# Three of eight key tiles of the full layers' value product as float32r pairs split on GpSimd, with feed normalisations and head splits on GpSimd too

## The chip, the cores and the metric

One Trainium2 chip, one core of it. The metric is the device time of one execution of the program in microseconds, lower is better. Every input is in float32 and the result is compared with a float32 reference.

## The reference

Four layers in a row work on `x` of 4 batches x 256 channels x 32 x 32 pixels, so 1024 tokens a batch.

```python
x = L0(x)   # gamma * attention(x) + x, q and k of 32 channels, v of 256
x = L1(x)   # x + wo(attention(group_norm(x))), q, k, v of 256 channels
x = L2(x)   # layer norm, causal attention with 8 heads of 32 and one shared k and v,
            # then layer norm, ff_w1, layer norm, gelu, ff_w2, residual
x = L3(x)   # as L1, with other weights
# attention of L0, L1 and L3 (the "full" layers), per batch:
scores = einsum('bci,bcj->bij', q, k) * scale      # 1024 x 1024
attn   = softmax(scores, axis=-1)
out    = einsum('bcj,bij->bci', v, attn)           # sum over 1024 keys j
```

## The kernel before, in words

Everything stays in SBUF. Three chains of work are woven together on every engine: the **full chain** (L0, L1 and L3 for four batches, 12 layers in all, in the order of the list `FULL`), the **causal chain** (the attention of L2 with its layer norm ahead) and the **feed chain** (L2's output product, norms and feed-forward part, in quarters of 256 tokens). A table of strings, `ORDER`, one per engine, says piece by piece which chain comes next: `F` or a digit is a piece of the full chain, `C` or a letter up to h of the causal one, `G` or a letter from i of the feed chain. On TensorE (the string `PE`) a digit or such a letter also names the PSUM bank of the eight in which the piece's result is put. A piece that opens a bank waits until the unit that held it has been read. The strings were put together ahead of time, nothing is decided at run time.

Most products are taken to float32 exactness by **pairs**: a float32 number is split into a float32r part (`hi`, rounded) and the rest (`lo`), and the product is three cheap float32r matmuls, hi x hi, hi x lo and lo x hi (`PASSES` and the helper `product`, line 758). ACT writes the hi part, DVE subtracts for the lo part. The attention's value product of a full layer is not done so, but as plain float32 matmuls, each of which the trace records as two instructions on TensorE (line 811, 768 in the program and 1536 in the trace).

A full layer goes, per query tile `ti` of 128 tokens: scores on TensorE (`full_scores`, two banks), row maximum on DVE (`row_max`, lines 1349 and 1352), exponential on ACT (`exponents`, line 1124), division on DVE (`invert`, line 1360), transposition on TensorE in two halves of four key tiles (`full_turn`, line 802, units t0 to t15), and copy of each half to `probsT` on ACT (`turned`, line 1132). After every second query tile comes a quarter of the values (`full_values`, units o0 to o3), which waits for the last of its four copies:

```python
for ct in range(CT):                      # 2 halves of the channels
    for j in range(NT):                   # 8 key tiles of 128
        last = mm(o[:, ct * QUARTER:(ct + 1) * QUARTER], vt[:, j, ct * P:(ct + 1) * P],
                  probsT[:, qi % (NQ - 1), j, :], start=j == 0, stop=j == NT - 1)
```

DVE then adds the quarter to the residual (`residual`, line 1370).

GpSimd (POOL) does 64 masks on the causal diagonal (`affine_select`, line 731) and 64 powers for the reciprocal roots of the norms (lines 710 and 720), nothing else of weight. DVE does the feed chain's normalisations (`norm_end` for the steps `f1b` and `f2b`, line 1557) and, as the third piece of `normalise`, divides a block of heads and splits it into a pair (lines 1672, 1675 and 1676).

Of the kernel before, what the change touches and what calls it, by code (L numbers as in the profile page):

```python
# [5 lines left out]
F32 = mybir.dt.float32  # L6
# [6 lines left out]
P = 128  # L13
# [28 lines left out]
        "0Fc4F60F2Fe50F72d5F401F756FFF3F750F26d7FFF0F2675d4FFF017FFF05F204F6F2046F012F405F710FFF2F456F012FFF3Ff70120F"  # L42
        "FF3F5F701F0FFF3fb3F53F705Fbh031F4h56FFF0F723fF6ah25dgFFaFbdfahce6F0123eegacd5gaFdFFbCaf71adeCgcbCe0jgdCfFFgF"
        "gdCjfpdbghCcjpeCc0ebCGceahce0cCdFC5kaC3f1F3fFfCakfaC5dakda5d5dfC1Fde76C3fCFb76nbC3Fgb5g1C2dfFdbFfdFfC2eFg04n"
        "gC6FcCGci4C50gCFcCFeCFgb2eCFg0C456pc0eFCcFCFhCC4CFcj6Fe03kj6Fa5GmFdFFgbh3if1F3ihf6F01kl4F2G6ad0F756FFcaehFca"
        "4F720Fd6e7caef7caFfFFdCca5F7301cfg3CaeFcnFCgFaf27Cd2FafpFaCFfalchfC6aeCa2F4o20Fe2gCFeo0ceGe2a5c0fCFgnC236fCF"
        "a520Flg52gClg3aFfpkCafFahGFfa2fFC0bfC14gCFca6C23eaFeCaFeageFaeC30ecFp5eCcC74cC2dCaC5FpFcCaepFcC0fCpkfF37fGC0"
        "fCFcC3CFCFfFmf2h22mF0pg246Fijcdf02dG6faFb034bF067FdbfaFdFb5F7adb03F56b7aFFdfFb2eF17gCe56c1FFhFc03eCg3FFcFbCe"
        "gaCdeoadCfahdcC4F0F64F0Fk64Fka67aC4F260F7e26ahCeFaeFhaFe0FcC62dCfC3F50jo2FFdFadCGac4F6aC23ae62FadeaFeCFga74C"
        "k0FbCFfFbCegibC6pe6F0ki64bGFg1aFe6beC16e1lgFdC764F3bC71oFoeC37e6CFpjcCFFGeC6bFa54bC6F5d12CFFF16dbCdFC512d4CC"  # L50
        "1FFFCg2Fie671dF0FpgFlF4dgamngd3G6adFb3505Fca74cfga2F4fgafhafa1f2FeCaf14af6cCFahFneCFca4cFC6a12eaFeC6i1ei6cbF"
        "feFCFcaC72aFgmib67C41Gc4gbFagFbFdC5bCFh4C3bm5F7bdCFbdFbCdFbdh13bd1fCF3afCaC15ibfC3bfFaCf2afa1fdfC1dfFp3eCfC7"
        "eCgCb4CopbCF36GibheCaCeCc0CgCFjCFoCF4Fop320F6Gm57FFF2F01m56p0FFjkF31G7FFF04F260F4F2604F326F014F326FFF0F724F3"
        "67FFF0F23456FFF707FFF"),
    "ACT": (
        "FFFFCFFFFFCCFFFCCFFFCCFFFFFFFFFCFFFFFCFFFFFFFFFFFFFFFFFFFFFFFFFFFCFFFFFFFFFFFFFCCFFFFFCCFFFFFFFFFFFFCCCCCCFC"
        "FFFFCCCCCFFCCCCCGCCCCGCGCCFFCCFFCFCFGCFFCFFCCCFFFCCFFFGCFFFCCCCFFFCGCFFFCCCCCCFFFFFFFCCCGCFCFCFGFFCGFGCFCFGF"
        "FFGFCCFFFFFCCCFFFCFFFCCCCCFFFFFCCCCFFCGCCCCFFFFGFCFFFCGFFCCCFFCFCFFGFFFFCGCGCCCFFFCCFFFCCCCCCCFFFFFFFCCGCCCC"
        "GCFFFCGCCCCFCFFGFFFFGFFFGCCCFFCFFFFCCCCCFFFFFFCCFFFFFCCFFCCCCCCCFFCFFFGFFFCFFFFFFFFFCCCCCCFFFGFFFCGCFFFFFCCC"
        "CFFCCCGFFFFGFCGFFFCFFCCFFFCGFFFCFFFCGCGCCFFFCCFFFCCCFFFFFFFCCFCFFCGFGCFGFCCCFFFFCFFCFCCCCFFFCCCFFFCCCCFFFCGF"  # L60
        "FFCCCCCGFFFFFFFGCCCCFFCFCCCFFFCCFCCFFFGCCCFFFCCCCFCCCFFGCGFCCCFCFCCGGFFFGFFFGFFFFFGFFGFFFFFFFFFFFFFFFFFFFFFF"
        "FFFFFFFFFF"),
    "DVE": (
        "CFFFFCFFFFFFCCFFCCFFCCCFFFFFFFCFFFFCFFFFFFFFFFFFFFFFFFFFFFFFFFFFFFCCFCFFFFFFFCCFFCCFFFFCCFCFFFFFCFFCCFCFFCCC"
        "CCFFCCCCCFFCCCCCCCCGGGCGGGCGCCGCCGGCCCGFFFCGCCFGCCFFCCFFFCCFGGGGGGFCGCCFFCGCFCFCCCGCCFGFGFCFFCGCFCCCCCFCCCFF"
        "FGGGGFGGGGCCCFFFFFCCGCFCCCFCGGFGCFGCGGGGCGGGCFGCCGCFGGFGFFGFFGFCCFCFCCCCCFFFFFFCCCCCFFFCFCCCCCCCGGGGGGFCGFCC"
        "CGCFCFFCFCCFFGFFFGCGFCGFCFFCCCFGFCCCFGGGFGGGFGFCGCFGGCGFCCGCCGFCCCFCFFCFFCCCCCCCFCFCCGGGFGGGFFGFFFFGCCCGGFGG"
        "CFCGCCCCCFGGGGGGFGCCGFFGGCFGFFCCGCCFGFCCFFCFCCCCFCFCFFCFCCFCFFCCCCCFCCCFCCCGCCCCCCFFGGGGFGFGFFGFFFGCFFGFFCGF"
        "CCCCCFCCFFFFGFFCCFCFCGFCCCCCCCFFGGGGGGGFCFFGFCFFGFFFGCGFCGFGCCFFCCFFCCCGGGFGGGFGFGFFGGFGGFCGCCFFFFFFFCCFFFFC"
        "FFFFCCCCFGGGCGGGCGCGGGFGCCCGCFGFFCCFCFFCCCCCFFCCCCFCFCCCCFCCCCGGGFGGGFGCCCFCFCGFCGGCCGCFFCFCFFFCGFCFFFCCGCCC"  # L70
        "FFGGGGGCCGCGCCFCCFCCCCFFFFCGCFCCCCCCFCCCFGGFGCCGCFGGGGFGGGGGGGCCGCFFGFFGGGGFGGGFGFGFGGGGFGFFFFFFFFFFFFFFFFFF"
        "FFFFFFFFFFFF"),
# [24 lines left out]
LN_SLOTS = 4  # L97

# [245 lines left out]
def build(nc, t):  # L344
# [38 lines left out]
    with ExitStack() as ctx:  # L383
# [36 lines left out]
        r_x, r_y, r_z, r_h, r_g, r_v, r_p, r_t = (region(k) for k in (8, 8, 8, 16, 16, 8, 8, 24))  # L420
# [124 lines left out]
        diag_masked = sem("diag_masked")  # L545
        full_step = sem("full_step")
# [151 lines left out]
        def _(pool):  # L698
# [3 lines left out]

            def full_chain():
                n = 0
                for l, b in FULL:
                    if l == "L0":
                        continue
                    n += 1
                    pool.wait_ge(gn_var_ready, n)
                    pool.tensor_tensor(gn_rstd[:, :], gn_var[:, :], half_neg[:, 0:CT], ALU.pow).then_inc(gn_rstd_ready, 1)  # L710
                    yield
# [32 lines left out]
        def _(pe):  # L744
# [61 lines left out]
            def full_values(l, b, qi):  # L806
                wait_read(pe, full_name(l, b, ("t", 4 * qi + 3)))
                o = open_unit(full_name(l, b, ("o", qi)))[:, 0, :]
                for ct in range(CT):
                    for j in range(NT):  # L810
                        last = mm(o[:, ct * QUARTER:(ct + 1) * QUARTER], vt[:, j, ct * P:(ct + 1) * P],  # L811
                                  probsT[:, qi % (NQ - 1), j, :], start=j == 0, stop=j == NT - 1)
                        if ct == CT - 1 and j == NT - 1:
                            last.then_inc(filled["f"], 1)
                        if j % TPH == TPH - 1:
                            yield
# [46 lines left out]
            def full_chain():  # L863
                for n, e in full_events():
# [25 lines left out]
                    else:  # L890
                        yield from full_values(l, b, e[1])
# [210 lines left out]
        def _(act):  # L1102
# [24 lines left out]
            def turned(l, b, ti):  # L1127
                for i in range(2 * ti, 2 * ti + 2):
# [3 lines left out]
                    nc.scalar.copy(probsT[:, ti // 2 % (NQ - 1), js, (ti % 2) * P:(ti % 2 + 1) * P],  # L1132
# [619 lines left out]
```

## Time and profile before

| | |
|---|---|
| time, median of 3 runs | 1383.28 us (1382.95 to 1383.52) |
| the profiled execution's own time | 1383.94 us |
| its span | 1382.2 us |
| TensorE's mean granted clock | 0.98 of 2.4 GHz |
| busy: PE, PEld, DVE, ACT, POOL | 1294.4, 1011.7, 846.2, 576.1, 92.2 us |
| idle time of PE | 1382.2 - 1294.4 = 87.8 us |

PE is TensorE's matmuls, PEld its weight loads (they overlap the matmuls). The duration of one matmul in the trace holds the way through the array, so that successive matmuls overlap: what one costs is the distance from its start to the next one's. The chain is the list of work, followed back from the last instruction, that set the end.

### The profile page before, as it was taken

To read this page: it belongs to the slowest core of one execution; us is meant where nothing else is said; L and a number is where in the kernel's file an instruction comes from. 1 tells how busy PE (TensorE), PEld (TensorE's weight loads), DVE (VectorE), ACT (ScalarE), POOL (GpSimd) and SP (SyncE) were. 2 spreads that over 40 slices of the span, in tenths; PEclk is the share of its full clock that TensorE was granted. 3 is DMA by queue.
4 is the path that set the end of the run, shared out by engine and by line. 5 is a ranking of instruction groups with operands and counts; after the bars stand their busy time and mean duration, and the time that the engine had idled before them with its cause. 6 is when DMAs were issued, how large, how long until landed. Compare 5 with 4: busy or idle time off the path is not lost.

```text
span 1382.2 us, 21753 instructions
## 1 busy us (share of the span) xinstructions
PE 1294.4 (94%) x8800; PEld 1011.7 (73%) x8800; DVE 846.2 (61%) x1886; ACT 576.1 (42%) x911; POOL 92.2 (7%) x134
## 2 busy tenths in 40 slices
PE   6979989899999898999999999999999999999898
PEld 5868777666768676776788767767787677668786
DVE  3634456787647757667477476676577676656451
ACT  3423343355343543544545245344435342453331
POOL 0000000110010001001100010001000000010000
PEclk9999999999999999999999999999999999999999
DMA  5000020110002000000020111000020101000000
GB/s 189 1 0 1 0 77 1 24 24 1 1 2 46 2 24 1 24 2 1 2 46 2 39 47 24 1 1 1 1 46 1 24 16 32 9 2 16 16 1 31
DMA packets 20610, 27.04 MB, mean 20 GB/s; under 512 B 3488, under 2 KB 14240, under 8 KB 20512
## 3 DMA queue, kind: packets, MB, share of 16 engines
q1 hardware_dynamic: 20512, 25.66, 6.6%
q8 instruction: 71, 1.16, 0.3%
q14 instruction: 27, 0.22, 0.1%
HBM read 8.61 MB, written 4.19 MB: 9 GB/s over the span
## 4 chain that ended last, share of the span: by engine, by line
PE 84%; DVE 8%; ACT 6%; issue 2%; DMA 1%; SPq 0%; ACTq 0%; DVEq 0%
PE ring L758 28%; PE ring L811 25%; PE ring L1062 10%; PE ring L1043 5%; PE ring L1026 4%; PE ring L802 4%; ACT probs L1124 1%; DVE part_max L1645 1%; PE ring L960 1%; PE ring L839 1%; PE ring L1030 1%; PE ring L995 1%; ACT probsT L1132 1%; DVE neg_max L1349 1%; DVE shift_max L1352 1%
## 5 line engine op out<-in xcount | busy, mean ns | idle before, releaser
L811 PE MATMUL ring<-probsT,vt 128*128 128x256 f32 x1536 | 359.7, 385 | 8.2 <-ACT probsT L1132 7.8
L811 PEld LDWEIGHTS ring<-probsT,vt 128*128 128x128 f32 x1536 | 287.5, 192 | 59.4 <-ACT probsT L1132 11.3
L1274 ACT ACTIVATE cprobs<-ring 128x1024 f32<-128x1024 f32 (+1 forms) x160 | 150.2, 941 | 252.5 <-PE ring L1043 251.5
L1124 ACT ACTIVATE probs<-ring,neg_max 128x1024 f32<-128x1024 f32 x96 | 107.0, 1115 | 148.0 <-DVE neg_max L1353 75.2
L1645 DVE TENSOR_REDUCE part_max<-ring 128x2 f32<-128x1024 f32 (+2 forms) x112 | 127.2, 1145 | 45.1 <-PE ring L1026 30.2
L1026 PE MATMUL ring<-ks,qs 96*128 96x512 f32 (+3 forms) x384 | 107.8, 379 | 11.1 <-DVE part_max L1645 4.1
L1043 PE MATMUL ring<-qs,ks 98*128 98x512 f32 x288 | 106.9, 443 | 9.8 <-ACT probs L1124 5.6
L1352 DVE TENSOR_REDUCE shift_max<-ring 128x1 f32<-128x1024 f32 x64 | 78.3, 1223 | 59.1 <-PE ring L758 57.0
L1132 ACT COPY probsT<-ring 128x512 f32<-128x512 f32 x192 | 101.9, 591 | 25.1 <-PE ring L802 25.1
L802 PE MATMUL ring<-consts,probs 128*128 128x128 f32 x768 | 107.6, 280 | 3.9 <-DVE probs L1360 1.5
L758 PE MATMUL ring<-h_hi,q_hi 128*128 128x512 f32 x256 | 107.4, 419 | 1.9 <-ACT vt L1146 0.7
L802 PEld LDWEIGHTS ring<-consts,probs 128*128 128x128 f32 x768 | 90.7, 144 | 23.6 <-issue 9.7
L758 PE MATMUL ring<-h_hi,q_lo 128*128 128x512 f32 x256 | 101.1, 395 | 0.0
L758 PE MATMUL ring<-h_lo,q_hi 128*128 128x512 f32 x256 | 100.6, 393 | 0.0
L1062 PE MATMUL ring<-cprobs,v 128*32 128x256 f32 (+1 forms) x1280 | 96.7, 374 | 0.1
L1062 PE MATMUL ring<-cprobs,ones 128*32 128x256 f32 (+1 forms) x1280 | 93.0, 362 | 0.0
L1026 PEld LDWEIGHTS ring<-ks,qs 96*128 96x128 f32 x384 | 61.6, 191 | 30.4 <-issue 7.4
L731 POOL TENSOR_SCALAR_AFFINE_SELECT cprobs<-cprobs 128x512 f32<-128x512 f32 x64 | 42.3, 662 | 558.5 <-ACT cprobs L1274 558.5
L1360 DVE TENSOR_SCALAR probs<-probs,row_inv 128x1024 f32<-128x1024 f32 x96 | 72.5, 756 | 3.4
L1043 PEld LDWEIGHTS ring<-qs,ks 98*128 98x128 f32 x288 | 49.2, 191 | 29.0 <-issue 15.3
L758 PEld LDWEIGHTS ring<-h_hi,q_hi 128*128 128x128 f32 x256 | 48.4, 189 | 19.5 <-issue 8.9
L1062 PEld LDWEIGHTS ring<-cprobs,v 128*32 128x32 f32 x1280 | 25.5, 108 | 45.9 <-issue 39.4
(226 smaller groups left out, 2110.1 us busy)
## 6 DMA issues: line engine op xcount, KB each, us to landing
qs<-q_hi SPq DMA_DIRECT2D x32, 128.0 KB, 2.3
qs<-q_hi SPq DMA_DIRECT2D x64, 64.0 KB, 2.0
x<-x_dram SPq DMA_DIRECT2D x3, 1024.0 KB, 6.1
qs<-q_lo SPq DMA_DIRECT2D x16, 128.0 KB, 2.3
qs<-max_rows SPq DMA_DIRECT2D x128, 2.0 KB
qs<-q_lo SPq DMA_DIRECT2D x32, 64.0 KB, 2.0
out_dram<-z SPq DMA_DIRECT2D x4, 512.0 KB, 2.8
out_dram<-x SPq DMA_DIRECT2D x4, 512.0 KB, 2.8
```

The source lines that it names most:

```text
L758: ins = mm(out, w, m, start=first and n == 0, stop=last and n == len(every) - 1)
L802: last = nc.tensor.transpose(o[:, j, :], probs[:, ti % 2, (TPH * hf + j) * P:(TPH * hf + j + 1) * P], ident)
L811: last = mm(o[:, ct * QUARTER:(ct + 1) * QUARTER], vt[:, j, ct * P:(ct + 1) * P], probsT[:, qi % (NQ - 1), j, :], start=j == 0, stop=j == ...
L1026: last = mm(o, stack(k, a, 3 * DH, at, at + P), ks[0:3 * DH, lo:hi], start=i % own == 0, stop=not diag and i % own == own - 1)
L1043: last = mm(heads(name)[:, a:a + own, 0:n], ks[0:3 * DH + 2, jt * P:(jt + 1) * P], stack(k, slice(a, a + own), 3 * DH + 2, QUARTER - n, QU ...
L1062: last = mm(acc[DH * a:DH * (a + 1), (half + 1) * QUARTER - n:(half + 1) * QUARTER], w, causal_probs(step, n)[:, a, :], start=jt == 0 and ...
L1124: A(probs[:, ti % 2, :], flat(full_name(l, b, ("s", ti))), ACT.Exp, bias=neg_max[:, ti:ti + 1], accum_out=row_sum[:, ti:ti + 1]).then_inc( ...
L1132: nc.scalar.copy(probsT[:, ti // 2 % (NQ - 1), js, (ti % 2) * P:(ti % 2 + 1) * P], slot(name)[:, 0, :].rearrange("p (s n) -> p s n", n=P)) ...
L1274: A(causal_probs(step, n), heads(name)[:, :, 0:n], ACT.Exp).then_inc(read_done[chain[name], "act"], 1)
L1352: full_then(v.tensor_reduce(shift_max[:, ti:ti + 1], flat(name), AX_X, ALU.max, negate=True))
L1360: v.tensor_scalar(probs[:, ti % 2, :], probs[:, ti % 2, :], row_inv[:, ti:ti + 1], None, ALU.mult).then_inc(probs_scaled, 1)
L1645: v.tensor_reduce(cols if ti < TPH else parts[:, ch, :], src[:, :, 0:n], AX_X, ALU.max, negate=True).then_inc(read_done["c", "dve"], 1)
```

## The change

1. In `full_values` the key tiles 3 to 7 stay plain float32 matmuls and come first; the key tiles 0 to 2 (`PAIRED = 3`) follow as pairs, three float32r matmuls each. Ahead of the first pair of a quarter TensorE waits for GpSimd's splits (`vt_split`, `probs_split`).
2. GpSimd makes these pairs: once a layer for `vt` (three key tiles, 768 numbers in a row of each partition), and once for each of the 8 query tiles for `probsT` (three key tiles, 384 numbers), always a copy that rounds to `hi`, a wait for it and a subtraction that writes `lo` over the source. It waits for ACT's copy of the first half of the query tile alone.
3. The normalisations `f1b` and `f2b` of the feed chain and the split of the divided heads go from DVE to GpSimd. (A function that would split the gelu there as well is defined and never called.)
4. The scratch tiles `turned_sums` and `den` are gone, both transpositions of `normalise` write to `nums`. `probsT` has two buffers in place of three.
5. The strings of `ORDER` are others, on all five engines.

```diff
 ORDER = {
     "PE": (
-        "0Fc4F60F2Fe50F72d5F401F756FFF3F750F26d7FFF0F2675d4FFF017FFF05F204F6F2046F012F405F710FFF2F456F012FFF3Ff70120F"
+        "0Fc4F60F2Fe50F72d5F401F760FFF3F516F021FFF3F0215ga1FFF027FFF03F513F5F0246F012F405F710FFF2F456F012FFF3fF70120F"
...
+PAIRED = 3
...
-        vt = shared("vt", [P, NT, C], r_v)
+        vt, vt_lo = (shared(n, [P, NT, C], r_v, d) for n, d in (("vt", F32), ("vt_lo", F32R)))
+        vt_hi = shared("vt_hi", [P, PAIRED, C], r_v + 8 * KIB, F32R)
...
-        probsT = shared("probsT", [P, NQ - 1, NT, QUARTER], r_t)
+        probsT, probsT_lo = (shared(n, [P, 2, NT, QUARTER], r_t, d) for n, d in (("probsT", F32), ("probsT_lo", F32R)))
+        probsT_hi = shared("probsT_hi", [P, 2, PAIRED, QUARTER], r_t + 16 * KIB, F32R)
...
+            def pair(hi, lo, src, step):
+                pool.tensor_copy(hi, src).then_inc(pair_step, 1)
+                pool.wait_ge(pair_step, step)
+                return pool.tensor_tensor(lo, src, hi.bitcast(F32), ALU.subtract)
...
+                    elif kind == "v":
+                        wait_read(pool, full_name(l, b, ("v", 0 if l == "L0" else (PAIRED - 1) // 2)))
+                        paired = slice(0, PAIRED)
+                        pair(vt_hi[:, :, :], vt_lo[:, paired, :], vt[:, paired, :],
+                             n * (NT + 1) + 1).then_inc(vt_split, 1)
+                    else:
+                        wait_read(pool, full_name(l, b, ("t", 2 * ti)))
+                        at = (slice(None), ti // 2 % 2, slice(0, PAIRED), slice((ti % 2) * P, (ti % 2 + 1) * P))
+                        pair(probsT_hi[at], probsT_lo[at], probsT[at],
+                             n * (NT + 1) + ti + 2).then_inc(probs_split, 1)
...
+            def normalised(b, name, src, t0):
+                n = norm_no[b, name]
+                at = n % LN_SLOTS
+                pool.wait_ge(rstd_ready["g"], n + 1)
+                for i in range(TPQ):
+                    ins = pool.tensor_scalar(an[:, t0 + i, :], src[:, t0 + i, :], ln_mv["g"][:, at, i, 0:1],
+                                             rstd["g"][:, at, i:i + 1], ALU.subtract, ALU.mult)
+                ins.then_inc(ln_ready["g"], 1)
+
+            def heads_split(b, k):
+                hg, qi = BLOCKS[k]
+                to = token_quarter(qi)
+                wait_read(pool, f"C{b}.o{k}")
+                split(b * K + k + 1, heads_out[0][:, hg, to], heads_out[1][:, hg, to],
+                      nums[:, hg, to]).then_inc(out_ready, 1)
...
-            def full_values(l, b, qi):
+            def full_values(l, b, n, qi):
                 wait_read(pe, full_name(l, b, ("t", 4 * qi + 3)))
                 o = open_unit(full_name(l, b, ("o", qi)))[:, 0, :]
                 for ct in range(CT):
-                    for j in range(NT):
-                        last = mm(o[:, ct * QUARTER:(ct + 1) * QUARTER], vt[:, j, ct * P:(ct + 1) * P],
-                                  probsT[:, qi % (NQ - 1), j, :], start=j == 0, stop=j == NT - 1)
...
+                    own, cs = o[:, ct * QUARTER:(ct + 1) * QUARTER], slice(ct * P, (ct + 1) * P)
+                    for j in range(PAIRED, NT):
+                        mm(own, vt[:, j, cs], probsT[:, qi % 2, j, :], start=j == PAIRED, stop=False)
+                    yield
+                    if ct == 0:
+                        pe.wait_ge(vt_split, n + 1)
+                        pe.wait_ge(probs_split, n * NT + 2 * qi + 2)
+                    last = product(own, [([w[:, j, cs] for w in (vt_hi, vt_lo)],
+                                          [p[:, qi % 2, j, :] for p in (probsT_hi, probsT_lo)]) for j in range(PAIRED)],
+                                   first=False)
...
                 elif kind == "f2b":
-                    yield from norm_end(b, f"f2.{hf}", an, t0, n, an)
                     return
...
-                    causal_then(v.tensor_copy(heads_out[0][:, hg, to], nums[:, hg, to]))
-                    v.tensor_tensor(heads_out[1][:, hg, to], nums[:, hg, to], f32(heads_out[0][:, hg, to]),
-                                    ALU.subtract).then_inc(out_ready, 1)
```

How the order of instructions moves is shown at three places. In these rows `x15` says that the row stands for 15 instructions alike.

TensorE, the first quarter of the values of the first layer (L0, batch 0), before. Line 789 is the scores, 802 the transpositions, 811 the values:

```order
L802 MATMUL ring<-consts,probs 128x128 [waits probs_scaled,full_act_read]
L802 MATMUL ring<-consts,probs 128x128 x3
L811 MATMUL ring<-probsT,vt 128x256 [waits full_act_read]
L811 MATMUL ring<-probsT,vt 128x256 x15
L789 MATMUL ring<-ks_57,qs_56 128x512 [waits full_act_read,causal_dve_read]
```

The same place with the change, where line 867 is the transpositions, 877 the plain values and 823 the pairs:

```order
L867 MATMUL ring<-consts,probs 128x128 x3
L877 MATMUL ring<-probsT,vt 128x256 [waits full_act_read]
L877 MATMUL ring<-probsT,vt 128x256 x4
L823 MATMUL ring<-probsT_hi,vt_hi 128x256 [waits probs_split,vt_split]
L823 MATMUL ring<-probsT_lo,vt_hi 128x256
L823 MATMUL ring<-probsT_hi,vt_lo 128x256
```

Sixteen plain products in one run became 5 plain, 9 of pairs, 5 plain, 9 of pairs, with the new wait after the first five.

GpSimd, in the middle of the program where the three chains meet, before (731 the diagonal's masks, 720 and 710 the roots):

```order
L720 TENSOR_TENSOR rstd_g<-var_eps_g,half_neg 128x2 [waits feed_var_ready] x2
L731 AFFINE_SELECT cprobs<-cprobs 128x4x128 [waits causal_act_read] x2
L720 TENSOR_TENSOR rstd_g<-var_eps_g,half_neg 128x2 [waits feed_var_ready]
L710 TENSOR_TENSOR gn_rstd<-gn_var,half_neg 128x2 [waits gn_var_ready]
L731 AFFINE_SELECT cprobs<-cprobs 128x4x128 [waits causal_act_read] x2
```

GpSimd with the change, a like place (788 the masks, 745 the roots, 758 the normalisations, 749 and 751 the split of heads, 711 and 713 a pair):

```order
L745 TENSOR_TENSOR rstd_g<-var_eps_g,half_neg 128x2 [waits feed_var_ready]
L758 TENSOR_SCALAR an<-xs,ln_mv_g,rstd_g 128x256 [waits feed_rstd_ready,causal_filled]
L758 TENSOR_SCALAR an<-xs,ln_mv_g,rstd_g 128x256
L711 CAST probsT_hi<-probsT 128x3x128 [waits full_act_read]
L713 TENSOR_TENSOR probsT_lo<-probsT,probsT_hi 128x3x128 [waits pair_step]
L749 CAST heads_out_hi<-nums 128x256 [waits causal_dve_read]
L751 TENSOR_TENSOR heads_out_lo<-nums,heads_out_hi 128x256 [waits split_step]
L745 TENSOR_TENSOR rstd_g<-var_eps_g,half_neg 128x2 [waits feed_var_ready]
L758 TENSOR_SCALAR an<-an,ln_mv_g,rstd_g 128x256 [waits feed_rstd_ready]
```

A queue of 128 short instructions with waits between them now holds 344 more (216 for pairs, 64 for normalisations, 64 for heads; the rest is the same), and a pair stands behind whatever of the two other chains was put ahead of it.

DVE, the first division of a block of heads, before:

```order
L1666 STREAM_TRANSPOSE turned_sums<-ring 128x256 [waits causal_filled]
L1668 RECIPROCAL inverse<-turned_sums 128x8 [waits causal_step]
L1669 STREAM_TRANSPOSE den<-inverse 128x256 [waits causal_step]
L1672 TENSOR_TENSOR nums<-ring,den 128x256 [waits causal_step]
L1675 CAST heads_out_hi<-nums 128x256 [waits causal_dve_read]
L1676 TENSOR_TENSOR heads_out_lo<-nums,heads_out_hi 128x256 [waits causal_step]
```

and with the change:

```order
L1735 STREAM_TRANSPOSE nums<-ring 128x256 [waits causal_filled]
L1737 RECIPROCAL inverse<-nums 128x8 [waits causal_step]
L1738 STREAM_TRANSPOSE nums<-inverse 128x256 [waits causal_step]
L1741 TENSOR_TENSOR nums<-ring,nums 128x256 [waits causal_step]
```

The cast and the subtraction left DVE's queue.

## Rows read from the trace of the kernel before

**Rows 1.** The page: busy time by engine, and the chain that ended last
```profile
PE 1294.4 (94%) x8800; PEld 1011.7 (73%) x8800; DVE 846.2 (61%) x1886; ACT 576.1 (42%) x911; POOL 92.2 (7%) x134
...
PE 84%; DVE 8%; ACT 6%; issue 2%; DMA 1%; SPq 0%; ACTq 0%; DVEq 0%
PE ring L758 28%; PE ring L811 25%; PE ring L1062 10%; PE ring L1043 5%; PE ring L1026 4%; PE ring L802 4%; ACT probs L1124 1%; DVE part_max L1645 1%; PE ring L960 1%; PE ring L839 1%; PE ring L1030 1%; PE ring L995 1%; ACT probsT L1132 1%; DVE neg_max L1349 1%; DVE shift_max L1352 1%
```

**Rows 2.** Groups of instructions of PE: busy us, mean ns, idle before
```profile
L811 PE MATMUL ring<-probsT,vt 128*128 128x256 f32 x1536 | 359.7, 385 | 8.2 <-ACT probsT L1132 7.8 <-DVE an L1611 0.4
```

**Rows 3.** Timeline of PE, 250 to 256 us: start, us, instructions in a row
```profile
252.87 1.89 PE L811 MATMUL ring<-probsT,vt 128*128 128x256 f32 x8
254.41 0.47 PE L758 MATMUL ring<-wo_hi,heads_out_hi 128*128 128x256 f32 x1
254.72 0.28 PE L758 MATMUL ring<-wo_lo,heads_out_hi 128*128 128x256 f32 x1
...
255.66 0.28 PE L758 MATMUL ring<-wo_hi,heads_out_hi 128*128 128x256 f32 x1
```

**Rows 4.** Waits of PE: total us, times, longest
```profile
PE ring L758 <- DVE h_lo L1424: 13.2, 1, 13.2
PE ring L811 <- ACT probsT L1132: 7.8, 8, 2.0
PE ring L839 <- issue: 7.3, 2, 3.7
```

**Rows 5.** Timelines of the last us: ACT's copies, and the last quarter's values
```profile
1369.14 1.04 PE L802 MATMUL ring<-consts,probs 128*128 128x128 f32 x8
...
1369.78 1.07 ACT L1132 COPY probsT<-ring 128x512 f32<-128x512 f32 x2 [8.41 <-PE ring L802]
...
1370.90 7.17 PE L811 MATMUL ring<-probsT,vt 128*128 128x256 f32 x32 [0.73 <-ACT probsT L1132]
```

**Rows 6.** POOL by line: count, ns min/median/max; then groups with busy us
```profile
L731 POOL TENSOR_SCALAR_AFFINE_SELECT cprobs<-cprobs x64: 634/635/1151, 218.4 to 1244.0; 128x512 f32<-128x512 f32 x64
...
L720 POOL TENSOR_TENSOR rstd_g<-var_eps_g,half_neg 128x2 f32<-128x2 f32 x48 | 36.2, 755 | 293.7 <-DVE var_eps_g L1539 293.5
```

**Rows 7.** DVE groups: what leaves the engine, and what stays beside POOL
```profile
L1676 DVE TENSOR_TENSOR heads_out_lo<-nums,heads_out_hi 128x256 fp32r<-128x256 f32 x32 | 14.2, 445 | 1.1
...
L1675 DVE CAST heads_out_hi<-nums 128x256 fp32r<-128x256 f32 x32 | 9.7, 303 | 1.1
...
L1557 DVE TENSOR_SCALAR an<-an,ln_mv_g,rstd_g 128x256 f32<-128x256 f32 x32 | 12.0, 419 | 2.0 <-POOL rstd_g L720 1.8
...
L1557 DVE TENSOR_SCALAR an<-xs,ln_mv_g,rstd_g 128x256 f32<-128x256 f32 x32 | 11.7, 409 | 5.5 <-POOL rstd_g L720 5.4
...
L1360 DVE TENSOR_SCALAR probs<-probs,row_inv 128x1024 f32<-128x1024 f32 x96 | 72.5, 756 | 3.4
```

**Rows 8.** DVE by line: count, ns min/median/max
```profile
L1675 DVE CAST heads_out_hi<-nums x32: 293/293/587, 248.9 to 1255.3; 128x256 fp32r<-128x256 f32 x32
...
L1424 DVE TENSOR_TENSOR h_lo<-h_full,h_hi x16: 1220/1225/1534, 93.7 to 1304.5; 128x1024 fp32r<-128x1024 f32 x16
```

**Rows 9.** Windows: us, busy PE, PEld, DVE, ACT, POOL, granted clock, DMA share, GB/s
```profile
350.00:450.00 100.00, 99.25 (x743) 77.57 (x742) 59.49 (x140) 39.32 (x56) 7.49 (x10) 1.00 0.07 17
450.00:550.00 100.00, 89.90 (x582) 67.88 (x580) 68.91 (x159) 43.26 (x68) 9.25 (x14) 0.93 0.04 9
```

More of the change, by code:

```diff
@@ L47 @@
[L47 to L51, printed above, removed]
@@ L68 @@
[L68 to L72, printed above, removed]
+        "FCFFFCFFFFFFCCFFCCFFCCCFFFFFFFFFFFCCFFFFFFFFFFFFFFFFFFFFFFFFFFFFFCFCFCFFFFFFFCCFFCCFFFFCCFCFFCCCCFFFFFCCCCFC"
@@ L701, in _, with pieces @@
             pool.wait_ge(setup, 2)
-            def full_chain():
[L704 to L710, printed above, removed]
+            def pair(hi, lo, src, step):
+                pool.tensor_copy(hi, src).then_inc(pair_step, 1)
+                pool.wait_ge(pair_step, step)
+                return pool.tensor_tensor(lo, src, hi.bitcast(F32), ALU.subtract)
+            def pieces(l):
+                return ([("gn", 0)] if l != "L0" else []) + [("v", 0)] + [("t", ti) for ti in range(NT)]
+            def full_chain():
+                start = {("gn", 0): ("t", 5)}
+                for n, (kind, ti) in full_order(pieces, {"L0": {}, "L1": start, "L3": start}):
+                    l, b = FULL[n]
+                    if kind == "gn":
+                        pool.wait_ge(gn_var_ready, normed(n))
+                        pool.tensor_tensor(gn_rstd[:, :], gn_var[:, :], half_neg[:, 0:CT],
+                                           ALU.pow).then_inc(gn_rstd_ready, 1)
+                    elif kind == "v":
[8 more added lines that the diff above has]
+                             n * (NT + 1) + ti + 2).then_inc(probs_split, 1)
                     yield
@@ L721, in root, with split, gelu_split @@
                                    ALU.pow).then_inc(rstd_ready[ch], 1)
+            def split(step, first, second, src):
+                pool.tensor_copy(first, src).then_inc(split_step, 1)
+                pool.wait_ge(split_step, step)
+                return pool.tensor_tensor(second, src, first.bitcast(F32), ALU.subtract)
+            def normalised(b, name, src, t0):
[12 more added lines that the diff above has]
+                      nums[:, hg, to]).then_inc(out_ready, 1)
+            def gelu_split(b, part):
+                first, second = act2[part % 2]
+                wait_read(pool, f"C{b}.tg{part}")
+                pool.tensor_copy(first[:, :, :], gelu[part % 2][:, :, :]).then_inc(gelu_rounded, 1)
+                pool.wait_ge(gelu_rounded, b * NQ + part + 1)
+                pool.tensor_tensor(second[:, :, :], gelu[part % 2][:, :, :], first[:, :, :].bitcast(F32),
+                                   ALU.subtract).then_inc(act2_ready, 1)
             def causal_chain():
@@ L726, in causal_chain @@
                         root(b, e)
+                        yield
+                    elif e[0] == "norm" and e[2] == NORM_PIECES - 1:
+                        heads_split(b, e[1])
                         yield
@@ L738, in feed_chain @@
                         root(b, e)
+                        yield
+                    if e[0] == "f1b":
+                        if e[1] == 1:
+                            wait_filled(pool, f"C{b}.vt1")
+                        normalised(b, f"f1.{e[1]}", xs, e[1] * TPQ)
+                        yield
+                    if e[0] == "f2b":
+                        normalised(b, f"f2.{e[1]}", an, e[1] * TPQ)
                         yield
@@ L890, in full_chain @@
                     else:
-                        yield from full_values(l, b, e[1])
+                        yield from full_values(l, b, n, e[1])
                         continue
@@ L1131, in turned @@
                     wait_filled(act, name)
-                    nc.scalar.copy(probsT[:, ti // 2 % (NQ - 1), js, (ti % 2) * P:(ti % 2 + 1) * P],
+                    nc.scalar.copy(probsT[:, ti // 2 % 2, js, (ti % 2) * P:(ti % 2 + 1) * P],
                                    slot(name)[:, 0, :].rearrange("p (s n) -> p s n", n=P)
```

78 lines of the change are left out of this document (43 added, 35 removed).

## The prediction

> **What bounds the kernel now.** I read the page first. TensorE is busy for 1294.4 of 1382.2 us, no other engine for more than 61%, and PE stands for 84% of the chain that set the end [rows 1]. Line 811, the plain float32 values that the change touches, is the second entry of that chain with 25% of the span, about 341 us, against 359.7 us of busy time in all [rows 1, 2]: 95% of this line's time lies on the path. So work taken from it shortens the end almost one for one, unless a wait comes in its place. PE's idle time is 1382.2 - 1294.4 = 87.8 us. The largest of its waits is the start, where nothing is loaded yet, and the next ones are of 7 to 8 us in several pieces [rows 4]; the rest is spread over some dozens of waits under 6 us each. The windows say the same: from 350 to 450 us PE is busy for 99% at the full clock, in the next 100 us for 90% at a mean clock of 0.93 [rows 9]. In the first kind of stretch PE's own work is the limit, in the second the way through ACT and DVE is.
>
> **TensorE's work.** The price of a matmul is the distance between starts. Eight plain instructions begin at 252.87, and the float32r product behind them has its second start at 254.72 [rows 3]: 1.85 us, which is 8 x 0.216 + 0.12. So a plain instruction costs 0.216 us, and going over to float32r costs nothing beyond. From 254.72 to 255.66 lie eight steps of float32r matmuls with the same 256 columns [rows 3], 0.118 us each; I take 0.120. One key tile of one channel half costs 2 x 0.216 = 0.432 us plain and 3 x 0.120 = 0.360 us as a pair, 0.072 us less. There are 12 layers x 4 quarters x 2 halves x 3 key tiles = 288: **-20.7 us**. With line 811's busy time over its count, 359.7 / 1536 = 0.234 us, which holds stretches at the lower clock and tails, it would be 288 x (0.468 - 0.360) = -31.1 us; with 0.216 and 0.125 it would be -16.4. On the path I count 95% of 20.7: **-19.7 us**.
>
> **GpSimd's splits.** The trace of before has neither a copy nor a plain subtraction on GpSimd. The nearest row is the mask with one input, 635 ns for 512 numbers a partition [rows 6], so 1.24 ns a number. For a copy of 384 numbers I take 384 x 1.24 = 0.48 us; for a subtraction with two inputs from once to twice that, 0.48 to 0.95 us, and take the upper end, because this engine may have to fetch them one after the other. The root with two numbers at 755 ns [rows 6] is another operation and only shows that a short instruction can be dear. A pair is 0.48 + 0.95 = 1.43 us, the bounds being 0.96 (both at the mask's rate) and 2.5 (both at that rate, each on top of the root's 0.755 as a fixed start). The Trainium skill, GPSIMD Engine Reference, section 3.1, gives 4497 ns for a two-input addition of 2048 numbers; by that the subtraction is 0.84 us and the pair 1.32, an estimate from that page, and no run here has shown it yet.
>
> In all: 96 pairs x 1.43 = 137 us, 12 pairs of `vt` with twice the size x 2.86 = 34, 32 splits of heads with 256 numbers x (0.32 + 0.63) = 30, 64 normalisations x 0.32 = 20. With the 92.2 us of before [rows 1] GpSimd has some 315 us, 23% of the span. It is no bound as an engine; what counts is when a pair is done.
>
> The quarter's last transpositions are followed by two copies in 1.07 us, and the values start at the end of the second, at 1370.90 [rows 5]. GpSimd may start after the first copy, about 0.54 us earlier. TensorE then does 5 plain key tiles, 10 x 0.216 = 2.16 us, ahead of the first one that needs the pair. So a pair has at least 0.54 + 2.16 = **2.7 us** even at the end of the program, where the chain runs alone, and needs 1.43 and a hand-over: covered, at 0. In the middle, where other chains' pieces stand ahead of it in GpSimd's queue, a split of heads (0.95) ahead still fits (2.4 us), two pieces ahead do not. Behind a mask that waits for its exponential the pair waits as well. I take 0 for it, the bounds being 0 and +30 (below). The split of `vt` is due only at the layer's first quarter, behind four transpositions and their softmax: hidden.
>
> **DVE.** It loses 14.2 + 9.7 + 12.0 + 11.7 = 47.6 us of 846 [rows 7], and with them the idle time ahead of the normalisations (5.5 + 2.0), since the root is made on GpSimd and the normalisation now follows it there. The new place costs nearly the same for a single piece (0.32 against 0.41 us, 0.95 against 0.75), so nothing behind it comes later. DVE stands for 8% of the chain [rows 1], 110 us; were 47.6 us of its 846 taken evenly, 6 us of the chain would go. I count 0, because most of what left was never waited for; the bounds are 0 and -8.
>
> **The rest.** The transposition into `nums` has the same shape. Two buffers of `probsT` suffice without a wait, since the transpositions of a quarter already stand behind the values of the quarter two before. No DMA is added or moved.
>
> **The order.** Every queue is reordered, and of its waits none can be read before the run. The pieces are the same, their neighbours are not. What the idle time can do is bounded by itself: of 87.8 us some 13 are the start, the other 75 may grow or shrink, and I take 0 with +-15, the two largest pieces of it after the start [rows 4]. Waits also move the clock: the mean of 0.98 says that 4% of the time, 55 us, ran at 1.2 GHz, and a stretch with more idle time is one with the lower clock [rows 9].
>
> **Sum:** -19.7 on the profiled execution's 1383.94 us gives 1364.2; the median of the runs lies 0.7 us under that execution, so 1363.6 us is forecast, 1.4% less.
>
> **Rivals.** (a) *Waits shrink as well.* With DVE lighter and the roots' hand-over gone, the waits of PE for DVE give back some 8 us, and the new order a few more: 1363.6 - 12 = about 1351. For it: much of the waiting is for DVE and ACT. Against: the list of waits is long and flat, no single one is removed. (b) *Half of the gain goes into waits.* Where PE is busy for 90% the path runs through ACT and DVE [rows 9] and a shorter value product only lengthens a wait; such stretches make up about half of the program: 1383.3 - 10 = 1373. For it: ACT's copies already end waits of the values [rows 4]. Against: 95% of line 811 is on the chain. (c) *No change.* GpSimd and DVE block one another. The cast of heads took 293 ns as a rule and 587 once, the subtraction for `h` 1225 and 1534, the mask 635 and 1151 [rows 6, 8]: one can hold the other up for some 0.3 to 0.5 us. GpSimd is busy for 23% of the time now instead of 7%. DVE has some 280 instructions that read or write SBUF alone (96 divisions of 0.75 us among them [rows 7]); a fourth of these held up for 0.3 us is 20 us, and if all of it landed on the path, the gain is gone: about 1384. Against: only 8% of the chain is DVE. The Trainium skill, SBUF — State Buffer, section "Who interferes with whom", says of this that VectorE and GpSimd share a port pair as an exclusive lock, for whole instructions; the longest durations above agree with it. (d) *Slower.* GpSimd's queue is late. A pair of 1.43 us, held up once (+0.5) and put behind a pair or another two pieces (+1.4), ends 3.35 us after the first copy, 0.65 too late; over 48 quarters that is +31 us, or 1363.6 + 31 = about 1395. It decides against the change from 3.2 us on: 0.47 us late on average over 48 quarters is 22.5 us. Against: 77% of GpSimd's time is free.
>
> **How the numbers follow.** The forecast's own case, 1354 to 1371, has 0.55; (a) 0.14, (b) 0.18, (c) 0.05, (d) 0.06; 0.02 is for a yet larger gain. A measurement of this kernel can tell 0.2%, 2.8 us, from no change. Faster by more than that are the forecast, (a), nearly all of (b) and the last: 0.88. Within it lie (c) and a little of (b): 0.06. Slower: 0.06. The range runs from (a)'s 1349 to 1378, past (b): some 0.83 of the cases.
>
> **What would show it.** The plain values should be 960 instructions and the pairs of `probsT` and `vt` 864, the first at 0.216, the second at 0.120 us from start to start, and PE's busy time near 1274. Waits of PE for the subtraction into `probsT_lo` should sum to under 5 us; over 20 is case (d). A pair on GpSimd should take 1.3 to 1.6 us, and all of GpSimd 290 to 340 us. PE's idle time should stay at 88 +- 15. The prediction is wrong if a pair takes over 2 us, or if idle time grows by as much as the busy time falls.

## The result and the profile after

The changed kernel takes 1387.32 us (median of 8 runs, 1383.07 to 1390.43) against 1383.85 us (8 runs) of the kernel before beside it: a ratio of 1.0026, 95% interval 1.0015 to 1.0037. It is slower by a quarter of a per cent where 1.4% less was forecast. The profiled execution was the fastest of the eight, 1383.07 us with a span of 1381.3 us, so its trace shows the loss of the gain, but not the last 4 us (its mean granted clock is 0.979, that of the other seven 0.970 to 0.975).

The page of the changed kernel, busy time and chain, to be read against [rows 1]:

```profile
PE 1271.4 (92%) x9088; PEld 1006.6 (73%) x9088; DVE 824.4 (60%) x1758; ACT 579.2 (42%) x911; POOL 406.6 (29%) x478
...
PE 79%; DVE 9%; ACT 5%; POOL 3%; issue 2%; DMA 1%; SPq 1%; ACTq 0%; DVEq 0%
```

PE's busy time fell by 1294.4 - 1271.4 = 23.0 us, as forecast (to about 1274). Its idle time rose from 87.8 to 1381.3 - 1271.4 = 109.9 us, by 22.1. Not quite two per cent of the work left TensorE and came back as waits. GpSimd has 407 us instead of the 315 reckoned.

The waits of PE, changed kernel (total us, times, longest; compare [rows 4]):

```profile
PE ring L823 <- DVE h_lo L1495: 17.4, 2, 14.4
PE ring L877 <- ACT probsT L1203: 11.7, 8, 3.2
...
PE ring L1031 <- DVE an L1628: 7.6, 2, 6.7
PE ring L1031 <- POOL an L758: 6.7, 6, 2.0
...
PE ring L1097 <- DVE part_max L1712: 4.3, 3, 3.8
...
PE ring L823 <- POOL heads_out_lo L751: 2.3, 2, 2.0
```

No row names `probsT_lo` or `vt_lo`: TensorE never sat idle for a pair. What is new are two long stalls, 6.7 us before line 1031 and 3.8 us before line 1097, both put down to DVE, and 9.0 us in 8 pieces for the pieces that moved to GpSimd. (The first two rows are longer than before as well, by 4.2 and 3.9 us. The 14.4 us are the start of the program, and both rows are as long in e7 below, one of the two fastest kernels, so they are not the loss.) So the question is what DVE waited for. The longest of the waits of DVE for GpSimd, changed kernel:

```profile
DVE gn_sc L1477 <- POOL gn_rstd L724: 19.3, 7, 7.4
```

`gn_rstd` is the root of the group norm of a full layer. Before, the same wait was 1.7 us in 2 pieces:

```profile
DVE gn_sc L1406 <- POOL gn_rstd L710: 1.7, 2, 0.9
```

The timeline of the changed kernel from 976 us shows one of them whole (start, us, instructions, in brackets the idle time ahead and what ended it):

```profile
976.71 0.16 DVE L1473 SCALAR_TENSOR_TENSOR gn_var<-gn_out,gn_sq 128x2 f32<-128x2 f32 x1
...
988.73 2.04 ACT L1203 COPY probsT<-ring 128x512 f32<-128x512 f32 x4
989.38 0.50 POOL L711 CAST probsT_hi<-probsT 128x384 fp32r<-128x384 f32 x1 [5.11 <-ACT probsT L1203]
989.96 0.99 POOL L713 TENSOR_TENSOR probsT_lo<-probsT,probsT_hi 128x384 fp32r<-128x384 f32 x1
990.92 0.70 POOL L724 TENSOR_TENSOR gn_rstd<-gn_var,half_neg 128x2 f32<-128x2 f32 x1
...
991.65 0.44 DVE L1477 TENSOR_TENSOR gn_sc<-gn_rstd,vecs 128x2 f32<-128x2 f32 x1 [7.37 <-POOL gn_rstd L724]
...
994.23 1.38 DVE L1628 TENSOR_SCALAR an<-xs,ln_mv_c,rstd_c 128x256 f32<-128x256 f32 x4
...
995.67 1.97 PE L1031 MATMUL ring<-consts,an 128*128 128x128 f32 x8 [6.69 <-DVE an L1628]
```

The variance is there at 976.87. GpSimd first had another root and two masks of the causal chain, then nothing to do for 5.1 us, but stood at the pair of query tile 5, whose copy ACT ended only at 989.3; the root stands behind that pair, by the table entry `start = {("gn", 0): ("t", 5)}`. DVE, in its own order, stood at the instruction that needs the root for 7.4 us, and behind it in DVE's queue was the causal chain's normalisation `an`, for which TensorE sat idle for 6.7 us. Nothing of this has to do with the pair's price; it is a queue whose head waits for something late, twice in a row. It meets just the three layers whose group norm is taken ahead (L3, batches 0 to 2): there the root begins 8.1, 14.1 and 9.2 us after its variance, and DVE stands for it for 4.1, 7.4 and 4.9 of the 19.3 us.

Each stall costs more than its own length, because TensorE runs at the lower of its two clocks just behind it. Windows of the changed kernel behind the stalls of 3.8 and 6.7 us (us, busy PE, PEld, DVE, ACT, POOL, granted clock, DMA share, GB/s):

```profile
634.90:636.80 1.90, 1.90 (x10) 1.90 (x9) 1.86 (x4) 1.51 (x2) 1.10 (x2) 0.50 0.00 0
996.00:999.00 3.00, 3.00 (x12) 2.73 (x11) 2.86 (x8) 1.15 (x2) 0.27 (x1) 0.50 0.00 0
```

A granted clock of 0.50 is 1.2 GHz. In the first of these windows a float32r matmul of 256 columns starts every 0.21 us; from 639.5 us on, at the full clock, every 0.12 us.

GpSimd's groups, changed kernel (busy us, mean ns), stand against the prices that were reckoned from [rows 6]:

```profile
L713 POOL TENSOR_TENSOR probsT_lo<-probsT,probsT_hi 128x384 fp32r<-128x384 f32 x96 | 98.9, 1030 | 7.9
L711 POOL CAST probsT_hi<-probsT 128x384 fp32r<-128x384 f32 x96 | 67.3, 701 | 330.5 <-ACT probsT L1203 330.4
...
L758 POOL TENSOR_SCALAR an<-xs,ln_mv_g,rstd_g 128x256 f32<-128x256 f32 x32 | 40.0, 1256 | 1.6 <-POOL rstd_g L745 0.4 <-PE ring L1114 0.2
...
L751 POOL TENSOR_TENSOR heads_out_lo<-nums,heads_out_hi 128x256 fp32r<-128x256 f32 x32 | 23.6, 736 | 2.7
```

A pair takes 1.73 us (1.43 reckoned), a split of heads 0.49 + 0.74 = 1.22 (0.95), but a normalisation of 256 numbers 1.25 us where 0.32 was reckoned: two of them, one for each of a piece's token tiles, are 2.5 us, against 0.82 on DVE [rows 7].

### The profile page after: what moved, and what is told of

The parts are those of the page before. It is cut to its first block, busy times and chain, and to the rows that moved or that the text cites. A ratio compares the mean times of both kernels' runs of the same rounds, so it can differ in the third digit from the quotient of the medians.

```text
span 1381.3 us, 22587 instructions
## 1 busy us (share of the span) xinstructions
PE 1271.4 (92%) x9088; PEld 1006.6 (73%) x9088; DVE 824.4 (60%) x1758; ACT 579.2 (42%) x911; POOL 406.6 (29%) x478
## 4 chain that ended last, share of the span: by engine, by line
PE 79%; DVE 9%; ACT 5%; POOL 3%; issue 2%; DMA 1%; SPq 1%; ACTq 0%; DVEq 0%
PE ring L823 35%; PE ring L877 14%; PE ring L1133 9%; PE ring L1114 5%; PE ring L1097 4%; PE ring L867 4%; ACT probs L1195 2%; PE ring L1031 2%; PE ring L910 1%; DVE part_max L1712 1%; POOL an L758 1%; DVE shift_max L1423 1%; ACT probsT L1203 1%; PE ring L1101 1%; POOL probsT_lo L713 1%
## 5 line engine op out<-in xcount | busy, mean ns | idle before, releaser
L877 PE MATMUL ring<-probsT,vt 128*128 128x256 f32 x960 | 230.0, 387 | 12.1 <-ACT probsT L1203 11.7
L877 PEld LDWEIGHTS ring<-probsT,vt 128*128 128x128 f32 x960 | 179.2, 194 | 41.0 <-ACT probsT L1203 14.6
L711 POOL CAST probsT_hi<-probsT 128x384 fp32r<-128x384 f32 x96 | 67.3, 701 | 330.5 <-ACT probsT L1203 330.4
L1114 PE MATMUL ring<-qs,ks 98*128 98x512 f32 x288 | 103.8, 433 | 9.5 <-DMA qs<-max_rows 4.1
L713 POOL TENSOR_TENSOR probsT_lo<-probsT,probsT_hi 128x384 fp32r<-128x384 f32 x96 | 98.9, 1030 | 7.9
L823 PE MATMUL ring<-probsT_hi,vt_hi 128*128 128x256 f32 x288 | 94.2, 327 | 0.0
L745 POOL TENSOR_TENSOR rstd_g<-var_eps_g,half_neg 128x2 f32<-128x2 f32 x48 | 36.7, 765 | 162.3 <-DVE var_eps_g L1610 162.0
L823 PE MATMUL ring<-probsT_lo,vt_hi 128*128 128x256 f32 x288 | 81.8, 284 | 0.0
```

The lines of the kernel that those rows point to most:

```text
L713: return pool.tensor_tensor(lo, src, hi.bitcast(F32), ALU.subtract)
L823: ins = mm(out, w, m, start=first and n == 0, stop=last and n == len(every) - 1)
L877: mm(own, vt[:, j, cs], probsT[:, qi % 2, j, :], start=j == PAIRED, stop=False)
L1114: last = mm(heads(name)[:, a:a + own, 0:n], ks[0:3 * DH + 2, jt * P:(jt + 1) * P], stack(k, slice(a, a + own), 3 * DH + 2, QUARTER - n, QU ...
```

## Experiments

Theories (the first four runs were made to tell N, O, L and P apart; H was tested from e6 on): **H**, the root of the group norm stands behind a pair in GpSimd's queue; **N**, the feed chain's normalisations are three times as slow on GpSimd and TensorE waits for them; **O**, the new order fits badly whatever GpSimd does; **L**, the pairs' own latency and hold-ups cost what they save; **P**, the pairs save their 20 us and all else costs as much. Every kernel was timed against the kernel before in alternation on one chip; the reference time beside them was 1384.45 (first four), 1382.66 (next four) and 1383.70 us (last). These references differ by up to 1.8 us, so that two kernels of different groups are compared more safely by their ratios.

| kernel | order | on GpSimd | root behind pair of tile | us | ratio to before, 95% |
|---|---|---|---|---|---|
| the change | new | pairs, norms, heads | 5 | 1387.3 | 1.0026 (1.0015 to 1.0037) |
| e1 | new | norms, heads | 5 (no pairs) | 1373.6 | 0.9917 (0.9900 to 0.9933) |
| e2 | new | pairs, norms cut to 1 column of 256, heads | 5 | 1379.5 | 0.9959 (0.9945 to 0.9973) |
| e3 | old | pairs | 4 | 1364.1 | 0.9856 (0.9836 to 0.9876) |
| e4 | new | pairs, heads | 5 | 1380.9 | 0.9966 (0.9948 to 0.9984) |
| e6 | new | pairs, norms, heads | 4 | 1372.7 | 0.9926 (0.9913 to 0.9939) |
| e7 | new | pairs, heads | 4 | 1359.0 | 0.9839 (0.9825 to 0.9853) |
| e8 | new | pairs | 4 | 1359.6 | 0.9835 (0.9814 to 0.9855) |
| e9 | old | pairs | 5 | 1385.4 | 1.0019 (1.0009 to 1.0028) |
| e10 | new | heads | 4 (no pairs) | 1369.7 | 0.9907 (0.9889 to 0.9925) |

### e1: the change without its pairs

```diff
-                        pair(probsT_hi[at], probsT_lo[at], probsT[at],
-                             n * (NT + 1) + ti + 2).then_inc(probs_split, 1)
...
-                    for j in range(PAIRED, NT):
-                        mm(own, vt[:, j, cs], probsT[:, qi % 2, j, :], start=j == PAIRED, stop=False)
...
+                    for j in range(NT):
+                        last = mm(o[:, ct * QUARTER:(ct + 1) * QUARTER], vt[:, j, ct * P:(ct + 1) * P],
+                                  probsT[:, qi % 2, j, :], start=j == 0, stop=j == NT - 1)
```

> The changed kernel without pairs: the values are plain float32 again (16 instructions a quarter and half), GpSimd makes no pairs; the new order and the work moved to GpSimd stay. Theory P (the pairs save their 20 us of PE and the rest of the change costs about as much): 1383.9 + 23 = about 1405 us, PE busy near 1294, PE idle 100 to 115. Theory L (the pairs' own latency or their hold-ups of DVE cost what they save, the rest is neutral): about 1384, PE idle near 90.

1373.6 us: both expectations missed. The new order with normalisations and heads on GpSimd is 11 us **faster** than before, and adding the pairs, which should take 20 us of work from TensorE (its busy time is 1287.9 us here, 1271.4 in the change), makes it 14 us slower. Theory P falls, and O with it as far as the order alone goes. Set against the changed kernel unit by unit on TensorE (the two have the same sequence outside the values), the lead that the pairs bring is 7.7 us by 625 us and is lost in jumps: 4.6 us at 633, 7.3 at 996 to 997, 2.5 and 1.5 at 1124 to 1129. These are the places of the three late roots. Smaller jumps of 1.2 to 2.1 us, at 412, 946, 1257 and 1283 us, stand where TensorE waits for a normalisation or a split of heads on GpSimd.

### e2: the normalisations on GpSimd cut to one column

```diff
-                    ins = pool.tensor_scalar(an[:, t0 + i, :], src[:, t0 + i, :], ln_mv["g"][:, at, i, 0:1],
+                    ins = pool.tensor_scalar(an[:, t0 + i, 0:1], src[:, t0 + i, 0:1], ln_mv["g"][:, at, i, 0:1],
```

> The changed kernel with the two normalisations of the feed chain on GpSimd cut to one column of 256 (the rest of the normalised rows is left out). Theory N (the new wait is the normalisation on GpSimd, 2 x 1.25 us where DVE needed 2 x 0.41, and the queue behind it): 1387 - 12 = about 1375 us or less, and the waits of PE for it (6.7 + a part of 7.6 us) gone. Theory O (the order taken over fits this kernel badly, whatever GpSimd does): 1384 to 1387.

1379.5 us, about 9 us or 0.67% less than the change by the two ratios (1.0026 against 0.9959). Theory N holds for a part: PE's wait for `POOL an` falls from 6.7 to 0.3 us. PE's 6.7 us stall ahead of line 1031 and its wait of 7.6 us in all for `DVE an` are unchanged, so that part has another cause. The run also shows what makes a normalisation on GpSimd dear (count, ns min/median/max):

```profile
L758 POOL TENSOR_SCALAR an<-xs,ln_mv_g,rstd_g x32: 364/374/387, 264.6 to 1278.4; 128x1 f32<-128x1 f32 x32
```

With one number in each partition it takes 0.37 us, with 256 numbers 1.23: 3.3 ns for each further number and 0.37 us whatever the size.

### e3: pairs alone, in the order of before

```diff
+                start = {("gn", 0): ("t", 4)}
...
-            def full_values(l, b, qi):
+            def full_values(l, b, n, qi):
...
+                    last = product(own, [([w[:, j, cs] for w in (vt_hi, vt_lo)],
+                                          [p[:, qi % 2, j, :] for p in (probsT_hi, probsT_lo)]) for j in range(PAIRED)],
+                                   first=False)
```

> The kernel before with its own order on PE, ACT, DVE and SP and only the pairs put in (GpSimd's queue gets them at the times at which ACT's copies ended in the trace of before; normalisations and head splits stay on DVE; the scratch tiles are laid on nums as in the change, to make room). Theory P or O: the 20 us of PE come out, 1384 - 20 = about 1364 (1359 to 1370). Theory L: no gain, 1380 or more, with waits of PE at the pairs.

1364.1 us, 1.44% less than before. The forecast's own sum for the pairs, -19.7 us, is what this kernel gives (-20.3). PE, e3:

```profile
PE 1272.8 (93%) x9088; PEld 1006.5 (74%) x9088; DVE 871.3 (64%) x1886; ACT 576.5 (42%) x911; POOL 288.1 (21%) x350
```

Busy time 21.6 us less, idle time 1364.3 - 1272.8 = 91.5 us, 3.7 more. Theory L is refuted in this order: 196 us of pairs on GpSimd, 14% of the span, cost next to nothing.

### e4: the normalisations back on DVE

```diff
                 elif kind == "f2b":
+                    yield from norm_end(b, f"f2.{hf}", an, t0, n, an)
                     return
```

In `ORDER`, 32 pieces leave GpSimd's string and are put in DVE's where, by the trace of the change, the root is ready.

> The changed kernel with the two normalisations of the feed chain back on DVE (placed where the root's end in the trace of the change allows), all else as changed. Theory N: 1387 - 12 = about 1375 us, as with the shortened normalisation. Theory O: 1384 to 1388, no change.

1380.9 us, the same as with the shortened normalisation within the intervals: 6.4 us less than the change by the medians, 8.3 by the ratios, a little over half of the 12 expected. The wait for `gn_rstd` stays:

```profile
DVE gn_sc L1470 <- POOL gn_rstd L725: 18.2, 7, 7.4
```

### e6: the root one pair earlier

```diff
-                start = {("gn", 0): ("t", 5)}
+                start = {("gn", 0): ("t", 4)}
```

> The changed kernel with one entry moved: in GpSimd's queue the group norm's root of L3's first three batches stands behind the pair of query tile 4 instead of tile 5 of the layer ahead. Theory H (head of line: the root waits behind a pair whose copy ends 8 to 14 us after the variance is there, DVE waits for the root with 19.3 us in 7 waits, TensorE stalls for 3.8 and 6.7 us): DVE's waits for the root fall to under 5 us and the time to 1387 - 12 = about 1375 us (1371 to 1379). Theory N (normalisations on GpSimd are the whole of it): 1384 to 1388.

1372.7 us, 14.7 us less than the change (13.8 by the ratios), from one entry of a table that changes no work. Theory H holds. The wait, e6:

```profile
DVE gn_sc L1477 <- POOL gn_rstd L724: 6.5, 6, 2.9
```

That is the value of the kernel without pairs, which has 6.6 us for it, not quite under the 5 expected. The lead over the change appears at the same three places: 4.1 and 1.6 us at 633 to 640, 6.7 and 1.6 us at 996 to 999, 1.5 and 1.5 us at 1124 to 1129. The first number of each is the stall, the second the stretch at 1.2 GHz behind it; e6 has the full clock at all three places.

One thing does not come back. With the normalisations on GpSimd and the root early the kernel with pairs (0.9926) is no faster than the one without (e1, 0.9917; the intervals overlap), although TensorE is busy for 18.5 us less and DVE's wait for the root is the same. A part of it stands in TensorE's waits for the normalisations, e1 first, then e6:

```profile
PE ring L1015 <- POOL an L748: 2.0, 3, 1.2
PE ring L1031 <- POOL an L758: 7.2, 6, 2.0
```

With the pairs the same normalisations are late for TensorE by 5 us more. Whether they end later, behind the pairs in one queue, or TensorE comes sooner because its own work is shorter, is not separated, and the rest of the 18.5 us is open.

### e7: root early, normalisations on DVE

The edits of e4 and e6 together.

> The same, and the feed chain's normalisations back on DVE. If the two causes are separate they add up: 1387 - 12 - 6.5 = about 1368 us. If they are the same waits seen twice: about 1375, as with the root alone.

1359.0 us, 28 us less than the change (26 by the ratios). The causes are separate and at least additive: 14.7 + 6.4 = 21.1 us by the medians, 13.8 + 8.3 = 22.1 by the ratios, and whether the 26 are more than that lies at the edge of the intervals. Set against e6, taking the normalisations off GpSimd is worth 12 us by the ratios (0.9926 against 0.9839). Without pairs e1 and e10 differ in the same way, and in the root's place, and lie within each other's intervals (0.9917 and 0.9907). So the longer instruction alone does not set the price: it costs where the pairs are there too. Of all kernels tried this is among the two best.

### e8: the head splits on DVE too

```diff
+                    causal_then(v.tensor_copy(heads_out[0][:, hg, to], nums[:, hg, to]))
+                    v.tensor_tensor(heads_out[1][:, hg, to], nums[:, hg, to], f32(heads_out[0][:, hg, to]),
+                                    ALU.subtract).then_inc(out_ready, 1)
```

> The same, and the split of heads back on DVE too, so that GpSimd has only pairs, masks and roots, in the new order. If the new order is as good as the one of before, about 1364 us as with pairs alone in the old order; if the head splits are better on GpSimd, some us more than the kernel with the normalisations alone on DVE (1368), since DVE then has 24 us more.

1359.6 us: no difference to e7. Taking the 24 us of splits from DVE or giving them back makes no difference that shows here; DVE's load is not the limit. It differs from e3 only in the order and the place of its pieces, and the two intervals, 0.9814 to 0.9855 and 0.9836 to 0.9876, overlap: with pairs, the new order is at most a little better than the old.

### e9: the old order with the root late

The edit of e6 the other way round, in e3.

> The old order with pairs (1364 us) with the same root put behind the pair of tile 5, as in the change. By the trace of that kernel the root would end 3.2, 4.6 and 7.7 us after DVE asks for it in the three layers. Theory H: DVE waits some 15 us for it and the time is 1364 + 6 to 12 = 1370 to 1376 us. If the root's place does not matter: 1362 to 1366.

1385.4 us: the whole gain of the pairs, 21 us, is gone by this entry alone, and more than the 6 to 12 us expected. DVE and PE, e9:

```profile
DVE gn_sc L1433 <- POOL gn_rstd L720: 17.0, 5, 7.7
...
DVE xs L1587 <- POOL rstd_g L741: 7.0, 7, 5.5
```
```profile
PE ring L823 <- DVE part_max L1672: 8.0, 1, 8.0
...
PE ring L1089 <- POOL cprobs L752: 4.9, 2, 2.9
```

DVE's 17.0 us for the root are the 15 worked out. What was not worked out is what stood behind in both queues: on GpSimd a root of the feed chain and the masks, on DVE a row maximum for which PE waited 8.0 us. Nor was the clock: TensorE's busy time is 1279.8 us against 1272.8 in e3, for the same instructions, so 7.0 of the 21 us are the same work taking longer, at a mean granted clock of 0.974 against 0.981.

### e10: e7 without pairs

The edits of e1 and e7 together.

> The kernel with the root early and the normalisations on DVE (1359.0 us) without its pairs, values plain again. If the pairs are worth in the new order what the distances between starts say, 20.7 us of TensorE, this is 1359 + 17 to 21 = 1376 to 1380 us. If the new order without pairs is itself what made 1359 (as the 1373.6 us of the changed kernel without pairs may suggest), it is under 1372.

1369.7 us. Here the pairs are worth 10.7 us by the medians (0.9907 against 0.9839, 0.7%, 9.4 us) and not 17 to 21, although the trace's busy time falls by 1286.5 - 1265.2 = 21.3 us. The profiled executions lie further apart (spans 1372.3 and 1357.1; that of e10 was the second slowest of its six). Where the missing part goes is not settled: TensorE's sequence shows steps of about 1 us, and the largest, 2.1 us at 413 us, is a wait for a split of heads on GpSimd, which e8 does not have without being faster. The second expectation, under 1372, came true: without pairs the new order is about 1% better than the old, with the heads on GpSimd. TensorE's busy time is 1286.5 us against 1294.4 before, for the same 8800 matmuls; why was not followed up.

## Why the prediction was wrong

**What bounds the kernel** held: TensorE's own work does, and pairs in the old order turned 21.6 us less busy time into 20.3 us less time.

**TensorE's work** held: 960 plain and 864 paired instructions at 216 and 120 ns (at the full clock) gave 23.0 us less busy time for 20.7 reckoned.

**GpSimd's splits**: price 1.43 us, measured 1.73, inside the bounds (0.96 to 2.5). The cover, 2.7 us, held: no wait of PE for a pair. The step that failed is in the same part, "Behind a mask that waits for its exponential the pair waits as well. I take 0 for it": I asked who may stand ahead of the pair, and never what stands **behind** it. The change's line `start = {("gn", 0): ("t", 5)}` put a root that DVE needs at once behind a pair whose input is not there, and the root began 8 to 14 us after its variance. It was to be seen before the run: in the trace of before all eight roots begin within 0.2 us of the end of their variance, and the order with the change has `gn_rstd` behind pairs. It costs 14.7 us by e6, and by e9 the same entry costs 21 in the old order.

**DVE**: "The new place costs nearly the same for a single piece (0.32 against 0.41 us ...), so nothing behind it comes later" failed as well. The mis-sized term is the normalisation on GpSimd; it measured 1.25 us. It was priced as one input at the mask's rate, though no row of before had such an instruction (two operations, with two scalars of each partition) on GpSimd. By e2 it has 0.37 us whatever its size and 3.3 ns a number; which of the two operations and two scalars makes it slow was not measured. With the root late the move is worth 6 to 9 us (e4 and e2), with the root early 12 to 14 (e7 against e6). The two failed steps together are 28.3 us by the medians, from 1387.3 to e7's 1359.0; the forecast of 1363.6 had them at nothing.

**The order**, taken as 0 +- 15: it was a gain of 11 to 14 us without pairs (e1, e10; both have the heads on GpSimd, e1 the normalisations too) and of some 3 to 4 us with them (e8 against e3, intervals overlapping), inside the bounds; why the gain shrinks with pairs is the part left open at e10. TensorE's idle time, 88 +- 15 forecast, came to 109.9 us, and grew by almost as much as the busy time fell, which the prediction had named as a sign that it is wrong.

**Rivals**: (d), about 1395 us, had the sign right and for its reason GpSimd's queue, but by pairs that come late to TensorE; those did not happen. (c), about 1384 us, lies nearest to the 1387.3 measured, and that is luck: what it goes by, the two engines holding one another up, is real, but e3 has it too (a mean of 673 ns for the cast) and keeps the whole gain. 59 of the 96 casts of `probsT` took 0.57 to 1.05 us instead of 0.50, and 57 of these overlap DVE's division of the probabilities. The cast, changed kernel (count, ns min/median/max):

```profile
L711 POOL CAST probsT_hi<-probsT x96: 498/804/1053, 39.3 to 1370.0; 128x384 fp32r<-128x384 f32 x96
```

That is 19.5 us more on GpSimd over the program. It agrees with the Trainium skill, SBUF — State Buffer, section "Who interferes with whom", that a `tensor_scalar` of VectorE can take the port pair that GpSimd needs, and that the other engine then waits. The Trainium skill, GPSIMD Engine Reference, section 3.1, has 2.6 cycles for a number of a two-input operation; an estimate from it, 384 x 2.6 cycles at 1.2 GHz, is 0.83 us, and the trace has 0.99 at least. The trace agrees with that rate, 2.17 ns a number: the shortest subtractions of 256, 384 and 768 numbers took 0.722, 0.992 and 1.822 us, 2.1 to 2.2 ns for each further number and some 0.17 us whatever the size.

## What to carry to other kernels

When work is put on an engine that so far served only short requests, list for each new piece that waits what stands behind it in that queue and who needs it: an idle engine (GpSimd at 21 to 30%) can hold up a busy one. Put a request that others wait for ahead of bulk work whose input comes later; here one entry of the table decided over 15 to 21 us. Two pieces of work that are each harmless alone on such an engine need not be so together: without the normalisations there the pairs gained 20 us in the old order and 9 to 11 in the new, with them nothing. And price an operation on another engine by a row of the same operation there, and where there is none, leave a wide bound.

## What the runs showed of the hardware

On GpSimd the cost a number depends strongly on the operation. The shortest casts took 0.397, 0.498 and 0.823 us for 256, 384 and 768 numbers, 0.8 ns for each further number; the subtraction with two inputs 2.1 to 2.2 ns; a subtraction and multiplication by per-partition scalars 3.3 ns, with 1.22 us for 256 numbers three times DVE's 0.41. The fixed part of the three is some 0.2, 0.17 and 0.37 us.

The float32r matmuls kept 120 ns and the plain ones 216 ns at the full clock when they alternate in runs of 9 and 10 (ten plain ones from 1001.62 us and the first step of the next run make up 2.28 us, to 1003.90).

After idle times of 3.8 and 6.7 us TensorE ran at 1.2 GHz (0.50 granted at 634.9 to 636.8 and 996 to 999 us), which made each of the two stalls dearer by some 1.5 us (the change against e6).
